# A scan kernel's GpSimd pacing: the wait names the VectorE instruction two places ahead of a multiply-add, not one, where the nearer one is a clip or a tap

## Chip, cores and metric

One Trainium2 chip, one of its cores. The metric is the device time of one launch in microseconds (us); lower is better.

## What is computed

Input x is 8 batches of 1024 tokens with 512 features, cond_2048 is one row of 1024 styles per batch. Two layers are added to x in turn. The first is a style-modulated attention of 16 heads. The second is a gated scan, and the change lies in it:

```python
xr, gate = jnp.split(x @ W_in.T, 2, axis=-1)
xr = xr + t_emb[:, None, :]
xc = silu(causal depthwise conv of 4 taps (xr) + b_conv)
xn = layernorm(xc) * ln_g + ln_b
Bm, Cm, dt = jnp.split(xn @ W_xproj.T, 3, axis=-1)
dt = jnp.tanh(dt @ W_dt.T + b_dt) * 0.01
Ad = 1.0 + dt * A
Bd = Bm * jnp.minimum(norm(xn), 1.0)
def step(h, inputs):
    ad, bd, xt, ct = inputs
    h = jnp.clip(h * ad[:, :, None] + bd[:, :, None] * xt[:, None, :], -10.0, 10.0)
    yt = jnp.einsum('bd,bdh->bh', ct, h)
    return (h, yt)
y = ys + D * xn
return y * silu(gate) @ W_out.T
```

The scan has 1024 steps, one after another; a step updates 16 states x 8 batches x 1024 channels.

## The kernel before

The attention layer comes first and the scan after it. The 8 x 16 pairs of batch and state lie on the 128 partitions, the 1024 channels along a row. The kernel stores h divided by the running product of its decays, so a step needs two VectorE instructions: the **multiply-add** (piece `q`, L2093, g <- xps * bd + g) and the **clip** (piece `g`, L2099, a TENSOR_SCALAR with a minimum and a maximum, in place on g). TensorE spreads the step's input row over the partitions ahead of it (`x`, L1807, into the PSUM tile xps, double buffered), and every fourth step multiplies four clipped states by the expanded C (`out`, L1822).

The 1024 tokens are cut in 8 chunks of 128. While the steps of chunk i run, the engines also prepare chunk i + 1 and finish chunk i - 1. On VectorE that side work is chiefly the **taps** (`tap`, L2106, three of the four of the convolution, each reading xr and cv from SBUF), small statistics (`mu`, `rs`, `rr`, `pjo` at L2161 and L2164, `nmin`, `nmul`) and the last add (`oo`, L2215). All of GpSimd's work in this stage is side work, in pieces of one TENSOR_TENSOR each: `a1`, `a2`, `a3`, `lo` (L2240, L2247, L2255, L2264; the affine part of the layer norm, D * xn, and the low part of a split), `ex` (L2233, the expansion of C, half as wide), `fy` and `fs` (L2272, L2284; the sum with D * xn and the gate). Each of these but `ex` comes as two halves of 512 columns.

The order of the instructions on every engine is laid down before the kernel is built, by the class Order. It keeps a clock of its own for each engine and, while the scan steps are placed, lets a GpSimd piece that is not overdue start only where it would begin within 0.2 of its own units after the start of a multiply-add. `self.open` holds the start of the latest multiply-add and, with it, the VectorE piece that is to be waited for; `place` writes the latter to `plan.pace`. The flag `port` marks the taps, the clips and all GpSimd pieces. When the instructions are emitted, `pace` adds the wait as the last of the piece's own waits:

```python
if p in self.plan.pace:
    for name in self.dve_signals(self.plan.pace[p]):
        w.wait_ge(self.sem[name], self.plan.after(name, self.plan.pace[p]))
```

The semaphores are dve_q for a multiply-add, dve_g for a clip, dve_tap for a tap. Of the 896 GpSimd pieces of the scan 691 are paced. The others follow on the piece before them with their data waits alone.

Of the kernel before, what the change touches and what calls it, by code (L numbers as in the profile page):

```python
# [48 lines left out]
class Plan:  # L49
# [3 lines left out]
    def __init__(self, nc, ctx, name):  # L53
        self.nc, self.ctx, self.name = nc, ctx, name
        self.pieces, self.place, self.counts, self.sems = [], {}, {}, {}
# [50 lines left out]
class Order:  # L106
# [5 lines left out]
    def __init__(self, plan, banks, lag):  # L112
        self.plan, self.lag = plan, lag
        self.now = dict.fromkeys(self.ENGINES, 0.0)
        self.free = dict.fromkeys(range(banks), 0.0)
        self.done, self.lanes, self.step = {}, [], -1

        self.port, self.open, self.before, self.late = {"DVE": 0.0, "POOL": 0.0}, None, None, None

    def lane(self, items, first=None, last=None):

        queues = {e: deque() for e in self.ENGINES}
        whole = sum(item["took"] for item in items) or 1.0
        sofar = 0.0
        for item in items:
            if first is not None:
                item["due"], item["side"] = first + (last - first) * sofar / whole, True
            sofar += item["took"]
            queues[item["engine"]].append(item)  # L130
        self.lanes.append(queues)
# [49 lines left out]
    def place(self, item, engine, start):  # L181
        plan, piece, group = self.plan, item["piece"], item["group"]
        if item["take"] is not None:
            m = min((m for m in item["take"] if self.free[m] is not None), key=lambda m: self.free[m])
            plan.bank[group], self.free[m] = m, None
        m = plan.bank.get(group)
        plan.put(piece, [(name.format(m=m), by) for name, by in item["signals"]])
        end = start + item["took"]
        if engine == "POOL" and self.late is not None and self.open is not None:
            plan.pace[piece], self.open = self.open[1], None  # L190
        if item["port"]:
            self.port[engine] = end
        if item["step"] is not None and engine == "DVE":
            self.open = (start, self.before)
        if engine == "DVE":
            self.before = piece
        self.now[engine] = end
        self.done[piece] = (engine if not item["lands"] else "DMA", end + item["lands"])
        if item["give"]:
            self.free[m] = end + self.lag[item["side"]]  # L200
        if item["step"] is not None:
            self.step = max(self.step, item["step"])
# [2174 lines left out]
```

## Time and profile before

| what | value |
|---|---|
| median of 3 runs | 6171.38 us (6165.83 to 6179.17) |
| profiled execution | 6177.47 us |
| its span | 6175.7 us |
| granted TensorE clock, mean | 0.968 |
| busy shares of the span: TensorE, VectorE, GpSimd, ScalarE | 93%, 73%, 52%, 39% |
| the 1024 steps | 3330.8 to 6087.0 us |

A busy share is the time in which an engine ran an instruction. A row of the timeline gives an instruction's start and duration, and in brackets how long its engine had idled before it and what ended that. An instruction that waits for the memory port while it is under way shows as a longer duration, not as idle time. Rows of the same kind that follow closely are merged (x2, x3), with the time from the first start to the last end.

### The profile page before, as it was taken

The numbers are of one execution on the slowest core, as the hardware profiler recorded it, in microseconds if no ns is written. First come the engines' busy times: TensorE is split into PE (matmuls) and PEld (weight loads), VectorE is DVE, ScalarE is ACT, GpSimd is POOL, SyncE is SP. The second block draws the span as 40 slices with busy tenths as digits, with TensorE's granted clock in tenths as the row PEclk, the third lists the DMA queues.
The fourth block names the chain that finished last, engine by engine and source line by source line (L and its number), as shares of the span: only waits on it lengthen the run. The fifth ranks groups of instructions, "written<-read, shape, count | busy, mean of one in ns | idle before, by whom it ended". The sixth has DMA issues, their size and how long they took to land.

```text
span 6175.7 us, 73238 instructions
## 1 busy us (share of the span) xinstructions
PE 5759.9 (93%) x24000; PEld 2733.8 (44%) x24000; DVE 4481.3 (73%) x5676; ACT 2408.7 (39%) x4698; POOL 3215.3 (52%) x2625
## 2 busy tenths in 40 slices
PE   7999999999999999999986879899999999999998
PEld 3444444444444444444443424444444444444444
DVE  4656656556566565665536999999989999989984
ACT  2444444445444444444453414333342424334111
POOL 1876767677667776776644333425243443524213
PEclk7999999999999999999988889999999999999999
DMA  2332323332232322323214343544444453444433
GB/s 86 89 92 69 100 74 93 91 88 86 79 96 78 98 81 74 98 76 86 91 48 128 84 116 99 141 101 131 109 119 130 117 137 90 137 101 130 116 96 118
DMA packets 411565, 613.30 MB, mean 99 GB/s; under 512 B 58768, under 2 KB 189968, under 8 KB 410672
## 3 DMA queue, kind: packets, MB, share of 16 engines
q1 hardware_dynamic: 374320, 558.24, 32.5%
q10 hardware_dynamic: 36864, 50.38, 3.2%
q8 instruction: 190, 3.11, 0.2%
q14 instruction: 191, 1.56, 0.1%
HBM read 305.31 MB, written 201.38 MB: 82 GB/s over the span
## 4 chain that ended last, share of the span: by engine, by line
PE 67%; DVE 19%; issue 6%; ACT 2%; ACTq 2%; DMA 2%; POOL 1%; DVEq 1%; SPq 1%; POOLq 0%
DVE g L2093 9%; PE bank L786 8%; PE bank L816 8%; PE bank L774 6%; PE misc L803 5%; PE miscb L1832 5%; DVE g L2099 5%; PE xps L1807 5%; PE miscb L1862 4%; PE yps L1822 4%; PE miscb L1764 3%; PE bank L745 3%; PE bank L727 3%; PE bank L755 3%; PE bank L803 2%
## 5 line engine op out<-in xcount | busy, mean ns | idle before, releaser
L1127 POOL TENSOR_TENSOR acc<-acc,prob 128x512 f32<-128x512 f32 x1536 | 1908.1, 1281 | 841.2 <-PE bank L816 571.2
L1056 DVE TENSOR_REDUCE mx<-bank 128x1 f32<-128x512 f32 x2048 | 1307.5, 684 | 538.7 <-PE bank L786 532.4
L2093 DVE SCALAR_TENSOR_TENSOR g<-xps,bd,g 128x1024 f32<-128x1024 f32 x1024 | 1312.9, 1282 | 111.4 <-PE xps L1807 84.1
L1807 PE MATMUL xps<-sx,spread 128*128 128x512 f32 x2048 | 890.3, 520 | 193.9 <-DVE g L2093 180.5
L949 ACT ACTIVATE prob<-misc 128x512 f32<-128x512 f32 x1277 | 713.5, 598 | 751.4 <-PE misc L803 667.8
L786 PE MATMUL bank<-khat,qhat 96*128 96x512 f32 x2048 | 939.4, 519 | 13.2 <-DVE xt_s L1033 8.0
L2099 DVE TENSOR_SCALAR g<-g,lim 128x1024 f32<-128x1024 f32 x1024 | 899.2, 878 | 34.9
L1807 PEld LDWEIGHTS xps<-sx,spread 128*128 128x128 f32 x2048 | 357.7, 194 | 679.3 <-issue 358.4
L803 PE MATMUL misc<-qhat,khat 98*128 98x512 f32 x1443 | 604.1, 461 | 16.9 <-ACT prob L949 10.7
L786 PEld LDWEIGHTS bank<-khat,qhat 96*128 96x128 f32 x2048 | 373.1, 191 | 540.8 <-issue 382.3
L1822 PE MATMUL yps<-g,cexp 128*32 128x512 f32 x4096 | 517.4, 625 | 0.0
L774 PE MATMUL bank<-xhT,wqk 128*128 128x512 f32 x1024 | 490.7, 606 | 2.6 <-ACT rsum L955 1.7
L816 PE MATMUL bank<-prob,V 128*32 128x512 f32 x3584 | 488.4, 615 | 0.2 <-ACT prob L949 0.2
L1764 PE MATMUL miscb<-x2T_sb,w_in 128*128 128x512 f32 x952 | 472.1, 606 | 12.0 <-DMA x2T_sb<-scratch_x2T 12.0
L1862 PE MATMUL miscb<-w_out,ygT 128*128 128x512 f32 x944 | 467.4, 604 | 0.3 <-ACT ygT L2033 0.3
L2233 POOL TENSOR_TENSOR cexp<-cd,mask 128x256 f32<-128x256 f32 x128 | 79.0, 617 | 713.7 <-DVE g L2099 448.5
L1832 PE MATMUL miscb<-w_in,x2T_t 128*128 128x512 f32 x896 | 439.6, 614 | 3.4 <-ACT xr L1912 1.8
L803 PEld LDWEIGHTS misc<-qhat,khat 98*128 98x128 f32 x1443 | 271.0, 190 | 254.0 <-issue 116.2
L2272 POOL TENSOR_TENSOR early<-early 128x512 f32<-128x512 f32 x118 | 150.4, 1275 | 444.1 <-DVE g L2099 244.5
L1047 DVE SCALAR_TENSOR_TENSOR halves<-bank,qk_dc,halves 128x512 fp32r<-128x512 f32 x128 | 95.3, 744 | 368.5 <-ACT halves L913 368.5
L1075 DVE RECIPROCAL rsum<-rsum 128x512 f32<-128x512 f32 x64 | 214.3, 3349 | 190.7 <-ACT rsum L955 190.7
L1912 ACT ACTIVATE xr<-miscb,temb 128x128 f32<-128x128 f32 x476 | 136.0, 369 | 533.5 <-PE miscb L1764 533.5
(221 smaller groups left out, 7212.6 us busy)
## 6 DMA issues: line engine op xcount, KB each, us to landing
sx<-scratch_xhl SPq DMA_DIRECT2D x512, 128.0 KB, 4.9
scratch_dx<-dx SPq DMA_DIRECT2D x64, 512.0 KB, 3.5
scratch_xhl<-xhi SPq DMA_DIRECT2D x64, 512.0 KB, 5.3
scratch_xhl<-xn SPq DMA_DIRECT2D x64, 512.0 KB, 5.6
scratch_y<-ysb SPq DMA_DIRECT2D x512, 64.0 KB
early<-scratch_dx SPq DMA_DIRECT2D x59, 512.0 KB, 6.2
early<-scratch_y SPq DMA_DIRECT2D x59, 512.0 KB, 4.3
xt_n<-in_x SPq DMA_DIRECT2D x112, 256.0 KB, 3.0
```

Of the source, the lines that this page charges most:

```text
L774: mm = pe.matmul(bank[m][:, 0:QC], self.wqk[:, n, it, :], self.xhT[:, it, c * QC:(c + 1) * QC], start=it == 0, stop=it == HT - 1)
L786: pe.matmul(bank[m][:, 0:QC], self.qhat[0:96, s, h, qt * P:(qt + 1) * P], self.khat[0:96, s, h, c * QC:(c + 1) * QC], start=True, stop=Tru ...
L803: pe.matmul(bank[m][:, 0:QC], self.khat[0:98, s, h, kt * P:(kt + 1) * P], self.qhat[0:98, s, h, c * QC:(c + 1) * QC], start=True, stop=Tru ...
L816: mm = pe.matmul(bank[6 + a][h * DH:(h + 1) * DH, 0:QC], self.value(b, kt, g)[:, h * DH:(h + 1) * DH], of, start=kt == 0, stop=kt == TT - 1)
L1056: dve.tensor_reduce(self.mx2[:, h * TT + qt, c:c + 1], bank[m][:, 0:QC], AX.X, ALU.max).then_inc(sem[f"dve_m{m}"], 1)
L1127: pool.tensor_tensor(self.acc[:, a, h, :], self.acc[:, a, h, :], self.prob[:, (n % 2) * GH + h, :], ALU.add).then_inc(sem["pool_acc"], 1)
L1807: mm = pe.matmul(self.xps[t % 2][:, half * BANK:(half + 1) * BANK], self.spread[:, 2 * part + half, :], self.sx[:, n % 2, wd, :], start=Tr ...
L1822: mm = pe.matmul(bank[2 + m][32 * j:32 * (j + 1), :], self.cexp[:, h, tc, :], self.g[:, (t + tp) % STATES, half * BANK:(half + 1) * BANK], ...
L1832: mm = pe.matmul(bank[m][:, :], self.room[rm]["x2T"][:, it, :], self.w_in[:, it, c:c + BANK], start=it == 0, stop=it == HT - 1)
L1862: mm = pe.matmul(bank[m][:, :], self.room[rm]["ygT"][:, ct, :], self.w_out[:, ct, :], start=ct == 0, stop=ct == CT - 1)
L2093: dve.scalar_tensor_tensor(self.g[:, t % STATES, :], self.xps[t % 2][:, :], self.bd[:, i % 2, tl:tl + 1], self.g[:, (t - 1) % STATES, :], ...
L2099: dve.tensor_scalar(self.g[:, t % STATES, :], self.g[:, t % STATES, :], self.lim[:, i % 2, 0, tl:tl + 1], self.lim[:, i % 2, 1, tl:tl + 1] ...
```

## The change

The planner now remembers, beside the last VectorE piece (`before`), the one ahead of it (`held`) where the last one is a clip or a tap. A multiply-add's entry names `held` if there is one.

```diff
@@ Order.__init__
         self.port, self.open, self.before, self.late = {"DVE": 0.0, "POOL": 0.0}, None, None, None
+        self.held = None
@@ Order.place
         if item["step"] is not None and engine == "DVE":
-            self.open = (start, self.before)
+            self.open = (start, self.held or self.before)
         if engine == "DVE":
+            self.held = self.before if item["port"] else None
             self.before = piece
```

Nothing in the choice of the next piece reads the name, so the order of instructions is the same on all five engines; only GpSimd's waits differ. Of the 691 paced pieces 520 named a clip. Of those 479 now name the multiply-add ahead of that clip, the one that the clip itself waits for; 19 name a projection (`pjo`), 18 a tap, 3 an output add, 1 a variance. Of the 65 that named a tap, 40 now name the tap ahead of it, 18 a clip and 7 a minimum.

GpSimd's rows, first a place within chunk 3 (in the trace it begins at 4499.38 us). Before:

```order
L2284 TENSOR_TENSOR early<-early,sg 128x512 [waits s_dve_g,s_pool_y0,s_act_m1]
L2240 TENSOR_TENSOR xn<-xn,affine 128x512 [waits s_act_nm]
L2240 TENSOR_TENSOR xn<-xn,affine 128x512 [waits s_dve_g]
L2247 TENSOR_TENSOR xn<-xn,affine 128x512 [waits s_dve_tap,s_pool_x] x2
L2255 TENSOR_TENSOR dx<-xn,affine 128x512 [waits s_dve_g,s_st_dx,s_pool_x]
L2255 TENSOR_TENSOR dx<-xn,affine 128x512 [waits s_dve_g,s_pool_x]
L2233 TENSOR_TENSOR cexp<-cd,mask 128x256 [waits s_dve_g,s_pe_y]
L2264 TENSOR_TENSOR xn<-xn,xhi 128x512 [waits s_pool_x,s_dve_tap,s_act_sq,s_act_hi]
L2264 TENSOR_TENSOR xn<-xn,xhi 128x512 [waits s_pool_x]
L2240 TENSOR_TENSOR xn<-xn,affine 128x512 [waits s_dve_g,s_act_nm]
L2240 TENSOR_TENSOR xn<-xn,affine 128x512 [waits s_dve_g]
```

After (the changed file's lines stand two further down):

```order
L2286 TENSOR_TENSOR early<-early,sg 128x512 [waits s_dve_q,s_pool_y0,s_act_m1]
L2242 TENSOR_TENSOR xn<-xn,affine 128x512 [waits s_act_nm]
L2242 TENSOR_TENSOR xn<-xn,affine 128x512 [waits s_dve_tap]
L2249 TENSOR_TENSOR xn<-xn,affine 128x512 [waits s_dve_g,s_pool_x]
L2249 TENSOR_TENSOR xn<-xn,affine 128x512 [waits s_dve_tap,s_pool_x]
L2257 TENSOR_TENSOR dx<-xn,affine 128x512 [waits s_dve_q,s_st_dx,s_pool_x]
L2257 TENSOR_TENSOR dx<-xn,affine 128x512 [waits s_dve_q,s_pool_x]
L2235 TENSOR_TENSOR cexp<-cd,mask 128x256 [waits s_dve_q,s_pe_y]
L2266 TENSOR_TENSOR xn<-xn,xhi 128x512 [waits s_pool_x,s_dve_tap,s_act_sq,s_act_hi]
L2266 TENSOR_TENSOR xn<-xn,xhi 128x512 [waits s_pool_x]
L2242 TENSOR_TENSOR xn<-xn,affine 128x512 [waits s_dve_q,s_act_nm]
L2242 TENSOR_TENSOR xn<-xn,affine 128x512 [waits s_dve_q]
```

No row has moved. Where dve_g stood there is dve_q in seven rows and dve_tap in one, and the number of waits of each of these rows is what it was: three for the first halves of `a3` and `fs`, two for `ex` and the second half of `a3`, one for the second half of `a1`.

VectorE's rows of a step, the same before and after:

```order
L2099 TENSOR_SCALAR g<-g,lim 128x1024 [waits s_dve_q]
L2093 SCALAR_TENSOR_TENSOR g<-xps,bd,g 128x1024 [waits s_pe_xps,s_dve_g]
L2099 TENSOR_SCALAR g<-g,lim 128x1024 [waits s_dve_q]
```

The clip's only wait is for dve_q, the semaphore that 479 GpSimd pieces now wait for too.

Among these 479 pieces 80 have that one wait alone (41 `a1`, 26 `fy`, 13 `ex`), 217 have two waits (39 `a1`, 64 `a2`, 36 `a3`, 14 `lo`, 64 `ex`), and 182 have three or four (41 `a3`, 73 `fs`, 44 `fy`, 24 `lo`).

## Rows read from the trace of the kernel before

**Rows 1.** The page: span, then busy us, share and instructions of engines.
```profile
span 6175.7 us, 73238 instructions
PE 5759.9 (93%) x24000; PEld 2733.8 (44%) x24000; DVE 4481.3 (73%) x5676; ACT 2408.7 (39%) x4698; POOL 3215.3 (52%) x2625
```

**Rows 2.** Windows: the steps; PE, PEld, DVE, ACT, POOL busy us, PEclk, DMA, GB/s.
```profile
3330.80:6087.00 2756.20, 2542.69 (x10754) 1208.58 (x10754) 2532.09 (x2747) 921.52 (x1926) 950.60 (x798) 0.97 0.43 113
```

**Rows 3.** Groups of VectorE and TensorE in the window of the steps.
```profile
L2093 DVE SCALAR_TENSOR_TENSOR g<-xps,bd,g 128x1024 f32<-128x1024 f32 x1024 | 1312.9, 1282 | 111.4 <-PE xps L1807 84.1 <-DVE g L2099 0.2
L2099 DVE TENSOR_SCALAR g<-g,lim 128x1024 f32<-128x1024 f32 x1024 | 899.2, 878 | 34.9
L1807 PE MATMUL xps<-sx,spread 128*128 128x512 f32 x2046 | 889.3, 520 | 180.8 <-DVE g L2093 180.5
```

**Rows 4.** VectorE's waits in that window: us in total, times, longest.
```profile
DVE g L2093 <- PE xps L1807: 84.1, 66, 9.4
DVE proj L2161 <- PE miscb L1783: 56.3, 24, 2.9
DVE x_t L2215 <- PE miscb L1862: 17.4, 13, 1.9
```

**Rows 5.** Timeline 4511 to 4518 us, VectorE and GpSimd.
```profile
4512.79 1.28 DVE L2093 SCALAR_TENSOR_TENSOR g<-xps,bd,g 128x1024 f32<-128x1024 f32 x1
4512.93 1.28 POOL L2255 TENSOR_TENSOR dx<-xn,affine 128x512 f32<-128x512 f32 x1 [0.80 <-DVE g L2099]
...
4514.11 0.81 DVE L2099 TENSOR_SCALAR g<-g,lim 128x1024 f32<-128x1024 f32 x1
...
4514.96 1.28 DVE L2093 SCALAR_TENSOR_TENSOR g<-xps,bd,g 128x1024 f32<-128x1024 f32 x1
4515.07 1.28 POOL L2255 TENSOR_TENSOR dx<-xn,affine 128x512 f32<-128x512 f32 x1 [0.86 <-DVE g L2099]
```

**Rows 6.** Timeline at 4526 us, a piece whose lone wait is the clip.
```profile
4526.49 1.28 DVE L2093 SCALAR_TENSOR_TENSOR g<-xps,bd,g 128x1024 f32<-128x1024 f32 x1
4526.53 1.28 POOL L2240 TENSOR_TENSOR xn<-xn,affine 128x512 f32<-128x512 f32 x1 [0.63 <-DVE g L2099]
```

**Rows 7.** Who waited for the clip, first and last of seven: us, times.
```profile
  POOL cexp L2233: 448.5, 71
...
  POOL dx L2255: 64.4, 70
```

**Rows 8.** Timelines at two places where clip and GpSimd start together.
```profile
3927.80 1.84 DVE L2099 TENSOR_SCALAR g<-g,lim 128x1024 f32<-128x1024 f32 x1
...
3927.81 1.27 POOL L2272 TENSOR_TENSOR early<-early 128x512 f32<-128x512 f32 x1
...
4849.58 1.93 DVE L2099 TENSOR_SCALAR g<-g,lim 128x1024 f32<-128x1024 f32 x1
4849.68 1.28 POOL L2284 TENSOR_TENSOR early<-early,sg 128x512 f32<-128x512 f32 x1
```

**Rows 9.** Timeline where GpSimd starts later than in rows 8.
```profile
3442.55 0.81 DVE L2099 TENSOR_SCALAR g<-g,lim 128x1024 f32<-128x1024 f32 x1
3442.69 3.04 POOL L2255 TENSOR_TENSOR dx<-xn,affine 128x512 f32<-128x512 f32 x2
```

**Rows 10.** Timelines of a clip behind an earlier full piece, and behind `ex`.
```profile
4524.63 1.27 POOL L2240 TENSOR_TENSOR xn<-xn,affine 128x512 f32<-128x512 f32 x1
...
4524.89 1.56 DVE L2099 TENSOR_SCALAR g<-g,lim 128x1024 f32<-128x1024 f32 x1
...
4642.69 0.61 POOL L2233 TENSOR_TENSOR cexp<-cd,mask 128x256 f32<-128x256 f32 x1
4642.95 0.90 DVE L2099 TENSOR_SCALAR g<-g,lim 128x1024 f32<-128x1024 f32 x1
```

## The prediction

> **What bounds the kernel now.** I read the page first: TensorE is busy for 93% of the span and VectorE for 73%, GpSimd for 52% [rows 1]. The change touches only the stage of the 1024 steps, so that stage has to be read by itself. Its window is 2756.2 us long; VectorE is busy for 2532.1 of it and TensorE for 2542.7, GpSimd for 950.6 [rows 2]. Two engines are thus full to 92%, and GpSimd has two thirds of its time free. What GpSimd does can cost time only by being late or by standing in another engine's way.
>
> Which of the two full engines waits for the other decides what a lost microsecond on VectorE costs. TensorE stood idle 180.5 us for the multiply-adds [rows 3]. VectorE waited 84.1 us in 66 waits for the rows that TensorE spreads, 56.3 us in 24 for the projections and 17.4 us in 13 for the output products [rows 4]; that is 158 us in 103 waits over 1024 steps. So in most steps VectorE waits for nobody: an undisturbed step is a multiply-add of 1.28 us, 0.03 to 0.04 us, a clip of 0.81 us and again 0.04 us, 2.17 us in all [rows 5], and a delay there moves every later step.
>
> The timeline shows how GpSimd is paced. The clip that starts at 4514.11 ends at 4514.92. The multiply-add follows at 4514.96, GpSimd's piece at 4515.07, and the two run side by side in 1.28 us each, neither one stretched [rows 5]. The piece ends at 4516.35, about 0.07 us into the next clip, which still takes its 0.81 us.
>
> How far GpSimd starts behind the multiply-add depends on how many waits its piece has, though the same clip releases both. With the clip as its lone wait it is 0.04 us [rows 6], with two waits 0.11 us, with three 0.14 us (4512.79 and 4512.93) [rows 5].
>
> **What the change does at a step.** It adds and removes no instruction of work and moves none. 479 pieces are released by the end of a multiply-add in place of the clip behind it. That same end releases the clip, and the clip's gap is the multiply-add's: 34.9 us over 1024 clips, 0.034 us [rows 3]. So I carry the three offsets over: the piece will start 0.04, 0.11 or 0.14 us behind a *clip*, with one, two, or three and more waits. Then it matters who gets the memory port.
>
> The rows show it. Where a piece starts 0.01 us or 0.10 us behind a clip, the clip takes 1.84 and 1.93 us in place of 0.81 and the piece its usual 1.27 or 1.28 [rows 8]: although the clip started first, GpSimd went first. In the steps 38 clips have a piece that starts up to 0.10 us behind them; all 38 were held, and the two places in rows 8 are the first and the last of them by offset. Where the piece starts 0.14 us behind, the clip keeps its 0.81 us and it is the piece that stretches (two pieces take 3.04 us) [rows 9]; that and 7 more clips with an offset up to 0.18 us were not held. The border lies between 0.10 and 0.14 us.
>
> The Trainium skill ("SBUF — State Buffer", section "SBUF: two separate sides") calls the shared pair of ports an exclusive lock: the instruction that starts first has it for its whole length and the other fully blocks. Of the blocking the trace agrees (1.93 in place of 0.81 us). Of who wins, the recorded starts disagree with it in all 38 cases.
>
> **The price of one held clip.** From rows 8, 1.84 - 0.81 = 1.03 us at 0.01 us and 1.12 at 0.10: 1.02 plus the offset. For the half-wide `ex` I compare at one offset: 0.26 us ahead of a clip, a full piece makes it 1.56 us and `ex` 0.90 [rows 10], so `ex` costs 0.66 us less.
>
> - One wait, offset 0.04: 67 full pieces at 1.06 and 13 `ex` at 0.40: 76 us. This offset lies well inside the held ones.
> - Two waits, offset 0.11: 153 at 1.13 and 64 at 0.47: 203 us. This lies 0.01 above the last held row and 0.03 below the first free one; I take it as held.
> - Three and more, offset 0.14: 182 at 1.16: 211 us. This lies at the first free row; I take it as not held.
>
> Not every piece is released by its pacing wait. The profile names the clip as what ended the wait of 467 pieces (seven rows, first and last in [rows 7]) of 520 that name one, 0.90. So 0.90 x (76 + 203) = 251 us.
>
> **What comes off.** The present conflicts cost (0.878 - 0.81) x 1024 = 70 us [rows 3]. Half of them are those 38 clips, hit by a piece that follows at once on a paced one. If the first of such a pair has three or four waits it now starts under the clip, blocked, and runs from the clip's end, about 0.3 us earlier than now. Its follower starts as much earlier and meets the next clip from 0.26 us ahead, which makes it 1.56 us in place of about 1.87 [rows 8, 10]: 38 x 0.3, some 10 us saved at the most. That leaves 241 us.
>
> **What is absorbed.** VectorE's 158 us of waits [rows 4] can swallow delays that came up before them, if TensorE goes on meanwhile; it cannot where it waits for the multiply-add itself. Nothing swallowed (241 us) and all 158 swallowed (83 us) are the bounds. The waits are few and the conflicts spread over all chunks, so I take a quarter: 181 us.
>
> Edits costed at nothing: the 19 clips after a projection, 18 after a tap and 3 after an output add do not wait for the piece named, and are under way when GpSimd comes; if they were held too, 40 x 1.1 = 44 us. The 18 that go from a tap to a clip come behind a tap that is under way likewise. The 40 with a tap behind a tap have offsets of 0.11 or 0.14 again, but no row shows who wins there; from nothing to 33 x 1.13 + 7 x 0.47 = 41 us. I take nothing and keep it for the top. GpSimd itself has two thirds of its time free, and nobody waits longer for its pieces than it now gains.
>
> **Sum.** The profiled execution took 6177.47 us; with 181 it is 6358, and the median is 6 us below that execution: 6352. I say 6350 us.
>
> **The rivals.**
>
> - *Only the lone waits collide* (the border is below 0.11 us). 0.90 x 76 - 10 = 58 us, less a quarter: 44 us, 6215 us. For it: no held row lies above 0.10 us.
> - *All collide* (the border is above 0.14 us). 0.90 x 490 = 441 us. The second pieces of pairs then find their clip over, which takes 38 x 1.06 = 40 off; three quarters of 401 is 301: 6472 us, and 6610 if nothing is swallowed. Against it: the clip was free at 0.14 us [rows 9].
> - *The clip always wins, the kernel is faster.* A clip and a piece released by one semaphore might be served in the order of their starts. Then no clip is lengthened, GpSimd starts at the clip's very end, 0.1 to 0.2 us earlier than now, and ends before the next clip begins. The gain is a part of the 70 us of conflicts; a third of it gives 6148 us, all of it 6101. This decides if no clip is held at 0.04 us. The skill's sentence above (first start has the port) is this rival, for 0.03 is less than 0.04. Against it stand all 38 rows.
> - *Nothing to be seen*: the pieces come after other waits so often, or the delays are swallowed so fully, that it stays at 6171 us. Against it are the 467 releases [rows 7] and the 103 waits only [rows 4].
>
> **How the numbers follow.** Two waits held and three not, my forecast: 0.5. Only lone waits: 0.2, all: 0.2, since the first has a fifth of the gap between 0.10 and 0.14 us below its offset and the last sits at the border. The clip wins: 0.06. Nothing: 0.04. The forecast's own range is 6270 (most swallowed, 83 us) to 6435 (nothing swallowed). The range reaches down to the lone-wait case, a little below 6215, and up through the middle of the all-held case: 6200 to 6510 us. It leaves out the two last rivals and the top of the second, some 2 in 10. A difference of under 0.2%, 12 us, can't be told from none here. Slower by more: 0.90; within: 0.05; faster by more: 0.05.
>
> **What the changed profile would show.** The clip's mean up from 878 ns: with 241 us more, to about 1110; to 935 if only lone waits collide, 1270 if all do, and below 878 if the clip wins. The second half of `a1` and of `fy` 0.04 us behind a clip of 1.87 us. Pieces with three waits stretched to about 1.8 us, with a clip of 0.81 us beside them. VectorE's 158 us of waits down by some 60, TensorE's 180.5 us of waiting for multiply-adds up. ScalarE and the 3330.8 us ahead of the steps as before. I am wrong at the root if clips keep 0.81 us beside a piece that starts 0.04 us behind them; wrong in size if the border is elsewhere or TensorE proves to be the real bound, so that more than half is swallowed.

## The result and the profile after

The changed kernel takes 6224.32 us (6213.63 to 6230.46), the kernel before 6172.0 us in the same comparison: a ratio of 1.0083, 95% interval 1.0065 to 1.01, 52 us slower. Slower was forecast, at 6350 us: the time lies in the range of 6200 to 6510, but the loss is less than a third of the 178 us that I gave. It lies 9 us above the first rival's 6215 us, and the range holds it only because it was stretched down to that rival: the forecast's own range began at 6270.

The page of the changed kernel, then its window of the steps (TensorE, weight loads, VectorE, ScalarE, GpSimd, granted clock, DMA, GB/s):

```profile
span 6228.6 us, 73238 instructions
...
PE 5796.9 (93%) x24000; PEld 2741.4 (44%) x24000; DVE 4527.1 (73%) x5676; ACT 2407.2 (39%) x4698; POOL 3436.1 (55%) x2625
```
```profile
3335.40:6140.60 2805.20, 2566.58 (x10756) 1212.76 (x10754) 2586.92 (x2746) 920.46 (x1926) 1172.97 (x798) 0.96 0.42 111
```

The window is 2805.2 us long; before it was 2756.2 [rows 2]: of the 52.9 us by which the span grew, 49 lie in it and 4.6 ahead of it. The start of the steps lies anywhere between 3321.5 and 3335.5 us in the eleven profiles, whatever the names. VectorE is busy for 54.8 us more there, GpSimd for 222 us more, and both engines ran the same instructions over the kernel.

The groups of the changed kernel in that window, with the same columns as [rows 3]:

```profile
L2095 DVE SCALAR_TENSOR_TENSOR g<-xps,bd,g 128x1024 f32<-128x1024 f32 x1024 | 1312.9, 1282 | 117.1 <-PE xps L1809 89.6
L2101 DVE TENSOR_SCALAR g<-g,lim 128x1024 f32<-128x1024 f32 x1024 | 954.4, 932 | 34.9
...
L1809 PE MATMUL xps<-sx,spread 128*128 128x512 f32 x2047 | 890.3, 521 | 208.3 <-DVE g L2095 207.3
```

The multiply-adds take what they took, and the gap ahead of the clips is the same 34.9 us. The clips alone grew, by 55.2 us, from 878 to 932 ns in the mean. TensorE waited 207.3 us for the multiply-adds, 27 us more than before. VectorE's waits for TensorE, to be held against [rows 4], add up to 153 us, 5 less than before:

```profile
DVE g L2095 <- PE xps L1809: 89.6, 68, 9.2
DVE proj L2163 <- PE miscb L1785: 50.0, 24, 2.9
DVE x_t L2217 <- PE miscb L1864: 13.0, 8, 2.1
```

Which clips grew is in the timeline. Three places of the changed kernel, VectorE and GpSimd:

```profile
4176.62 0.81 DVE L2101 TENSOR_SCALAR g<-g,lim 128x1024 f32<-128x1024 f32 x1
4176.75 1.82 POOL L2257 TENSOR_TENSOR dx<-xn,affine 128x512 f32<-128x512 f32 x1 [0.23 <-DVE g L2095]
...
4178.78 0.81 DVE L2101 TENSOR_SCALAR g<-g,lim 128x1024 f32<-128x1024 f32 x1
4178.89 1.85 POOL L2257 TENSOR_TENSOR dx<-xn,affine 128x512 f32<-128x512 f32 x1 [0.32 <-DVE g L2095]
...
4190.45 1.88 DVE L2101 TENSOR_SCALAR g<-g,lim 128x1024 f32<-128x1024 f32 x1
4190.49 1.29 POOL L2242 TENSOR_TENSOR xn<-xn,affine 128x512 f32<-128x512 f32 x1 [0.27 <-DVE g L2095]
```

All three pieces were released by the end of a multiply-add. With three waits (the first half of an `a3`) the piece starts 0.13 us behind the clip (4176.75), with two (the second half) 0.11 us (4178.89): the clip keeps its 0.81 us, and the piece is the one that stretches, from 1.28 to 1.82 or 1.85 us. With one wait (the second half of an `a1`) it starts 0.04 us behind the clip (4190.49): the clip takes 1.88 us. Over the whole kernel 69 clips have a piece 0.04 us behind them and are held, and of the 283 with an offset of 0.105 to 0.135 us not one is. The last held offset of the two kernels is 0.098 us, the smallest free one 0.105.

The balance of the clips, each against 0.81 us: the 69 cost 65.6 us. The clips held by a follower 0.01 to 0.10 us behind them fell from 38 to 6, those held by a piece that had started ahead of them or otherwise rose from 44 to 69; together these two give 10.4 us back. 65.6 - 10.4 = 55.2 us.

### The profile page after: what moved, and what is told of

Read it like the earlier page. It is cut to its first block, busy times and chain, and to the rows that moved or that the text cites. A ratio compares the mean times of both kernels' runs of the same rounds, so it can differ in the third digit from the quotient of the medians.

```text
span 6228.6 us, 73238 instructions
## 1 busy us (share of the span) xinstructions
PE 5796.9 (93%) x24000; PEld 2741.4 (44%) x24000; DVE 4527.1 (73%) x5676; ACT 2407.2 (39%) x4698; POOL 3436.1 (55%) x2625
## 4 chain that ended last, share of the span: by engine, by line
PE 62%; DVE 23%; issue 6%; ACT 2%; ACTq 2%; DMA 2%; POOL 1%; DVEq 1%; SPq 1%; POOLq 0%
DVE g L2095 11%; PE bank L788 8%; PE bank L818 8%; DVE g L2101 6%; PE bank L776 6%; PE misc L805 5%; PE miscb L1834 4%; PE xps L1809 4%; PE yps L1824 3%; PE bank L747 3%; PE miscb L1864 3%; PE bank L729 3%; PE bank L757 3%; DVE cv L2108 2%; PE miscb L1766 2%
## 5 line engine op out<-in xcount | busy, mean ns | idle before, releaser
L1809 PE MATMUL xps<-sx,spread 128*128 128x512 f32 x2048 | 890.8, 521 | 221.2 <-DVE g L2095 207.3
L2101 DVE TENSOR_SCALAR g<-g,lim 128x1024 f32<-128x1024 f32 x1024 | 954.4, 932 | 34.9
L2235 POOL TENSOR_TENSOR cexp<-cd,mask 128x256 f32<-128x256 f32 x128 | 116.7, 912 | 674.4 <-DVE g L2095 415.3
L2274 POOL TENSOR_TENSOR early<-early 128x512 f32<-128x512 f32 x118 | 170.6, 1448 | 425.2 <-DMA early<-scratch_y 244.4
```

What stands on the lines that cost most here:

```text
L1809: mm = pe.matmul(self.xps[t % 2][:, half * BANK:(half + 1) * BANK], self.spread[:, 2 * part + half, :], self.sx[:, n % 2, wd, :], start=Tr ...
L2101: dve.tensor_scalar(self.g[:, t % STATES, :], self.g[:, t % STATES, :], self.lim[:, i % 2, 0, tl:tl + 1], self.lim[:, i % 2, 1, tl:tl + 1] ...
```

## The experiments

Two facts of the code are needed for them.
**Without the lone waits (e1).** `near` holds the name of before. Here and below only the lines that decide are shown.

```diff
         if p in self.plan.pace:
-            for name in self.dve_signals(self.plan.pace[p]):
-                w.wait_ge(self.sem[name], self.plan.after(name, self.plan.pace[p]))
+            named = self.plan.pace[p] if w.fresh else self.plan.near[p]
+            for name in self.dve_signals(named):
+                w.wait_ge(self.sem[name], self.plan.after(name, named))
```

> The changed kernel, but a piece whose pacing wait would be its only wait keeps the name of before (the clip); all others are as changed. First theory: the whole loss comes from lone-wait pieces that start 0.04 us behind a clip and take the port from it (69 held clips, some 55 us of clip time). Then no clip is held at 0.04 us, the clip's mean is back at 870 to 885 ns and the time at 6160 to 6180 us. Rival: the loss comes from the 300 pieces with two and more waits, which now start under a clip and run on from its end, so that their followers meet the next clip from ahead; then the time stays within 15 us of 6224.

6152.38 us, ratio to before 0.9979 (0.997 to 0.9988). The clip's mean was 869 ns. The first theory holds and its rival falls: the other pieces that now name the multiply-add, 217 with two waits and 182 with more, cost nothing. They even gain 17 us, so that the time lies 8 us below the range expected.

**The offset alone (e2, e9).** All names as changed; only the lone pieces get one more wait, on a load that landed long ago.

```diff
         if p in self.plan.pace:
+            if not w.fresh:
+                w.engine.wait_ge(self.sem["ld_const"], 48)
             for name in self.dve_signals(self.plan.pace[p]):
```

> The changed kernel with one more wait, long satisfied (on the constants' load), called ahead of the pacing wait where that was the only one. First theory: the offset decides. The pacing wait then stands in an instruction of its own and the piece starts 0.11 us behind the clip in place of 0.04; it loses the port, no clip is held there, 6155 to 6180 us, clip mean 865 to 885 ns. Rival: naming the multiply-add costs by itself, whatever the offset: 6224 us.

6151.16 us, ratio 0.9972 (0.996 to 0.9983), against 6224 without the extra wait. The second half of an `a1` in this kernel, a piece of the kind that starts at 4190.49 above:

```profile
4162.01 0.81 DVE L2104 TENSOR_SCALAR g<-g,lim 128x1024 f32<-128x1024 f32 x1
4162.12 1.84 POOL L2246 TENSOR_TENSOR xn<-xn,affine 128x512 f32<-128x512 f32 x1 [0.33 <-DVE g L2098]
```

0.11 us in place of 0.04, and the clip keeps its 0.81 us. An added wait that is already met thus makes the kernel some 72 us faster (6222.99 us for e3, run beside it): the offset decides, not the name. One thing stays open. In e2, e3 and e5 the offset changes together with the instruction that holds the pacing wait, so for pieces that wait the two are not told apart. For the offset itself speak the followers, which wait for nothing when they start: they are held from 0.01 to 0.10 us and free from 0.14 us on.

**The same wait at the other place (e3).** It is called behind the pacing wait.

```diff
             for name in self.dve_signals(self.plan.pace[p]):
                 w.wait_ge(self.sem[name], self.plan.after(name, self.plan.pace[p]))
+            if w.fresh == 1:
+                w.engine.wait_ge(self.sem["ld_const"], 48)
```

> As the run with the satisfied wait ahead, but it is called behind the pacing wait, so the pacing wait stays the one that the work instruction itself holds. If what counts is which wait the instruction holds, these pieces still start 0.04 us behind the clip, the 69 clips stay held and the time is 6215 to 6235 us. If the number of waits counts, the offset is 0.11 us and the time 6155 to 6180 us.

6222.99 us, ratio 1.0091 (1.0076 to 1.0106), the changed kernel's time. In this kernel:

```profile
4184.09 1.88 DVE L2104 TENSOR_SCALAR g<-g,lim 128x1024 f32<-128x1024 f32 x1
4184.14 1.29 POOL L2246 TENSOR_TENSOR xn<-xn,affine 128x512 f32<-128x512 f32 x1 [0.26 <-DVE g L2098]
```

As many waits as in e2, yet the offset is 0.04 us (0.042 to 0.044 before rounding). What counts is not how many waits a piece has but where the pacing wait stands among them.

**The lone pieces alone (e4).** The names of e1 the other way round.

```diff
+            named = self.plan.near[p] if w.fresh else self.plan.pace[p]
```

> The opposite part alone: only pieces whose pacing wait is their only wait name the instruction two places ahead, all others the clip or tap as before. First theory: about 69 clips held at 0.04 us, 57 full ones at 1.06 us and 12 half-wide ones at 0.40, 65 us of clip time less what else shifts: 6220 to 6240 us. Rival (the others cost): 6172 us.

6234.63 us, ratio 1.0111 (1.0096 to 1.0126), as expected. 88 clips were held by a piece 0.04 to 0.06 us behind them, against 26 in the kernel before, and the clips took 957.2 us against 899.2. Here the others name the clip again and do not give their small gain, which is why I take this kernel to be slower than the changed one, by 12 us against e3. The loss of the lone pieces is some 65 to 73 us, seen from either side.

**All pieces at 0.04 us (e5).** `pace` is called ahead of every other wait of the piece.

```diff
         for p in plan.pieces:
             kind, *at = p
+            self.pace(w, p)
...
-                self.pace(w, p)
```

> The changed kernel with the pacing wait called first for every GpSimd piece, so that the work instruction itself holds it, however many waits the piece has. If that wait is what makes the piece start 0.04 us behind the clip, nearly all 430 to 479 clips are now held: against the changed kernel 0.9 x (335 x 1.06 + 64 x 0.40) = 340 us more of clip time, mean near 1250 ns, and with a tenth of it swallowed about 6530 us (6450 to 6570). It also measures how much of a large delay TensorE's slack swallows: a quarter would give 6480, nothing 6565. Rival (the number of waits sets the offset): 6224 us, clip mean 932 ns.

6532.67 us, ratio 1.0589 (1.0573 to 1.0605). This is what it costs when all collide: it lies between the 6472 us of that rival and its 6610. It is also what was expected of the run. The piece is at 0.04 us although it has two or three waits, and both prices of the prediction can be read off. A half-wide `ex`, then a full `fs`:

```profile
4151.54 1.21 DVE L2101 TENSOR_SCALAR g<-g,lim 128x1024 f32<-128x1024 f32 x1
4151.58 0.62 POOL L2235 TENSOR_TENSOR cexp<-cd,mask 128x256 f32<-128x256 f32 x1 [12.48 <-DVE g L2095]
...
4174.30 1.87 DVE L2101 TENSOR_SCALAR g<-g,lim 128x1024 f32<-128x1024 f32 x1
4174.34 1.28 POOL L2280 TENSOR_TENSOR early<-early,sg 128x512 f32<-128x512 f32 x1 [1.95 <-DVE g L2095]
```

1.87 - 0.81 = 1.06 us and 1.21 - 0.81 = 0.40 us, as priced. 363 clips were held at 0.04 us. The groups and waits of this kernel in the steps (waits: us in total, times, longest):

```profile
L2101 DVE TENSOR_SCALAR g<-g,lim 128x1024 f32<-128x1024 f32 x1024 | 1247.5, 1218 | 34.9
L2108 DVE SCALAR_TENSOR_TENSOR cv<-xr,wconv,cv 128x512 f32<-128x512 f32 x336 | 296.9, 884 | 7.5 <-ACT cv L1924 0.9
```
```profile
DVE g L2095 <- PE xps L1809: 70.6, 49, 9.1
DVE proj L2163 <- PE miscb L1785: 52.8, 24, 3.0
DVE x_t L2217 <- PE miscb L1864: 10.9, 6, 1.9
```

Clips took 348 us more than before [rows 3] and taps 40 us more (296.9 against 257.0 in the kernel before). VectorE's waits for TensorE fell from 158 us [rows 4] to 134: of 388 us 24 were swallowed, 6%. The time agrees, 365 us more.

**Naming the unpaced pieces too (e6).** As e2, and a piece that follows at once on another names the latest multiply-add placed (`self.last`).

```diff
-        if engine == "POOL" and self.late is not None and self.open is not None:
-            plan.pace[piece], self.open = self.open[1], None
+        if engine == "POOL" and self.late is not None:
+            if self.open is not None:
+                plan.pace[piece], self.open = self.open[1], None
+            elif self.last is not None:
+                plan.pace[piece] = self.last
```

> The changed kernel with the satisfied wait ahead of lone pacing waits, and with a pacing wait for the pieces that have none now (they follow at once on the piece before): they name the latest multiply-add placed. No clip should then find a piece that started 0.26 us ahead of it or 0.04 behind it. The 73 other held clips of the changed kernel cost some 60 us of clip time; if most of them go, the clip's mean falls to 815 to 840 ns and the time to 6110 to 6140 us, below both kernels. Rival: pieces that wait become late, and TensorE and the output products wait for them; then 6170 us or more, with VectorE's or TensorE's waits up.

6147.71 us, ratio 0.9965 (0.9952 to 0.9978). The fastest of the first six by its median, but within the spread of e1 and e2, and not the 6110 to 6140 expected. The clip's mean fell to 849 ns only: 54 clips still meet a piece that started about 0.26 us ahead of them. Such a place, shown in e2, where it occurs likewise:

```profile
4179.59 0.81 DVE L2104 TENSOR_SCALAR g<-g,lim 128x1024 f32<-128x1024 f32 x1
4179.73 1.81 POOL L2290 TENSOR_TENSOR early<-early,sg 128x512 f32<-128x512 f32 x1
...
4181.50 1.28 POOL L2261 TENSOR_TENSOR dx<-xn,affine 128x512 f32<-128x512 f32 x1
4181.76 1.57 DVE L2104 TENSOR_SCALAR g<-g,lim 128x1024 f32<-128x1024 f32 x1
```

The first piece is stretched by a clip and ends at 4181.54; the next, whose release is past, is recorded from 4181.50, just as that one ends. This is 0.26 us ahead of the next clip, and that takes 1.57 us.

**One multiply-add for each piece (e7).** In the same place; `self.prior` is the name of the piece before.

```diff
+            named, self.open = (self.open[1], None) if self.open is not None else (self.last, None)
+            if named is not None:
+                if self.prior is not None and plan.place[named] <= plan.place[self.prior]:
+                    named = self.last
+                plan.pace[piece] = self.prior = named
```

> The kernel in which all pieces are named, with one rule more: a piece whose name lies no later in the plan than the name of the piece before it names the latest multiply-add placed. In the version without the rule 54 clips are still hit by a piece that started about 0.26 us ahead of them. Theory: these are pieces behind a backlog; their name was long past, so they started on the heels of the piece before. With the rule they wait for a multiply-add of their own: held clips 10 to 30, clip mean 820 to 835 ns, VectorE 15 to 30 us shorter, 6115 to 6135 us. Rival: GpSimd's pieces then come later and the waits of TensorE and VectorE for the chunk's side work grow by as much: 6140 to 6155 us with a clip mean just as low.

6177.5 us, ratio 1.0012 (1.0003 to 1.0021): slower than e6 by some 30 us, and not as expected. The clip's mean did fall, to 835 ns, but the taps gave it back, and VectorE waited more. First e6, then e7, in the steps:

```profile
L2108 DVE TENSOR_SCALAR g<-g,lim 128x1024 f32<-128x1024 f32 x1024 | 869.1, 849 | 34.9
L2115 DVE SCALAR_TENSOR_TENSOR cv<-xr,wconv,cv 128x512 f32<-128x512 f32 x336 | 263.4, 784 | 6.3
```
```profile
L2109 DVE TENSOR_SCALAR g<-g,lim 128x1024 f32<-128x1024 f32 x1024 | 855.0, 835 | 34.9
L2116 DVE SCALAR_TENSOR_TENSOR cv<-xr,wconv,cv 128x512 f32<-128x512 f32 x336 | 282.9, 842 | 6.9 <-ACT cv L1932 0.6
```

Clips 14 us less, taps 19.5 us more: 33 taps were held in the steps, against 13. VectorE's waits for the rows of TensorE rose from 89.3 to 99.4 us, and 7.8 us of waits for ScalarE's sum of squares are new. That is 5.4 us of clips and taps and 18 us of waits; some 6 of the 30 us stay unexplained. Neither theory had the time. The rival named the waits, which are the larger part, and nobody the taps. Which of the later pieces met which tap I did not follow up.

**Is it the names that gain? (e8, e9).** e8 is the kernel of before with e2's three lines; e9 is e2 again, on the same chip.

> The kernel of before, all names as they were, with the satisfied wait ahead of lone pacing waits. Theory: the 18 us that the changed names gain once the lone pieces no longer take the port come from the names, so here nothing moves: 6160 to 6176 us, clip mean 870 to 885 ns. Rival: they come from the 0.07 us later start of the lone pieces; then this kernel too is at 6145 to 6155 us.

> The changed names with the satisfied wait ahead once more, beside the kernel of before with that wait, to have both on one chip: 6145 to 6160 us, and 10 to 25 us below the other.

e8: 6164.32 us, ratio 0.9993 (0.9984 to 1.0002), no difference. e9: 6146.67 us, ratio 0.9969 (0.996 to 0.9979), 18 us below e8. So the changed names gain about 0.3% once no lone piece takes the port from a clip, and the extra wait gains nothing by itself.

## Why the prediction was right in its mechanism and wrong in its size

- **"The piece will start 0.04, 0.11 or 0.14 us behind a clip"**: right. After, they start 0.04, 0.11 and 0.13 us behind it. The offsets carry over from the multiply-add to the clip.
- **The lone waits, 80 pieces, 76 us**: right. 69 clips were held, at 1.06 us a full piece and 0.40 an `ex` (e5), 65.6 us in all. With the cut of 0.90 the term was 68 us; e1, e2 and e4 put it at 65 to 73 us of time.
- **"Two waits, offset 0.11: ... I take it as held"**: this step failed. The term of 203 us was nothing: the pieces with two waits came 0.11 us behind the clip, and all those clips kept their 0.81 us. The offset stood 0.01 us above the last held row and 0.03 below the first free one, and I went by the nearer row. No row of before lay in that gap; the border is between 0.098 and 0.105 us. The nearer row was also of another kind, a piece that followed on its predecessor without idling, while the pieces of this term are released by a wait. Without this term the sum is the first rival's, 44 us against the 52 measured. The forecast's 0.5 against 0.2 for the right case came from treating the border as equally likely anywhere in it.
- **Three and more waits, not held**: right. They were free at 0.13 us, and e5 shows that the same pieces are held when they come at 0.04.
- **What comes off, 10 us**: right, 10.4 us in the changed kernel. In e2, where only this is left, the clips' mean falls from 878 to 861 ns, 17 us, while the taps take 6.5 us more. The followers now meet a clip from 0.26 us ahead (1.57 us) and not from 0.01 to 0.10 behind (1.84 to 1.93). That kernel gains 19 us (e2) and 23 us (e9) against before; the 11 us of clips and taps explain half, and what makes up the rest stays open. Within the steps VectorE idled 2 us less in the profile of e2 and 12 us less in that of e9.
- **"I take a quarter"** as swallowed: too much. From before to after the clips grew by 55 us and the steps by 49, and VectorE's waits fell by 5 us, not by the 60 foretold; in e5 VectorE gave up 24 us of waits for 388 us of delays, where a quarter would be 97.
- **Two sums are off.** The bounds of 83 and 241 us on the median of 6171 give 6254 and 6412, not 6270 and 6435. And the 6610 of the second rival leaves out the 40 us that its 6472 takes off; with them it is 6572. Neither moves the forecast.
- **The taps behind a tap, taken at nothing**: right for the changed kernel; those with an offset of 0.11 and 0.13 us kept their 0.75 us, one `ex` at 0.045 us held its tap to 1.21 us, and the taps' total in the steps is 257.6 us against 257.0. In e5, where the same offset is 0.04, they took 40 us more.
- **The rival in which the clip always wins, and the sentence of the Trainium skill** ("SBUF — State Buffer", section "SBUF: two separate sides") that who starts first has the port: 0.04 us behind, GpSimd still went first, 69 times here and 363 times in e5. That one of the two waits for the other holds, though not to the full recorded length: the clip from 4190.45 ends 0.55 us after the piece, less than its own 0.81, and the piece from 4178.89 ends 1.15 us after its clip, less than its own 1.28. The order of the recorded starts is not the order in which the two were served; that turns over at about 0.1 us.

## What to carry to other kernels

When two engines are released by one event and contend for one port, ask not only who starts first but by how much: here a few hundredths of a microsecond decided about 1 us a clip. The place of a wait among an instruction's waits sets that offset, so a long satisfied wait ahead of the pacing wait can buy it: here it turns 52 us lost into some 20 us won. Where a forecast hangs on a border that the trace brackets only loosely, its two sides are two forecasts, and the nearest row counts only if it is of the same kind.

## What the runs showed of the hardware that I had not expected

- A GpSimd piece starts 0.079 us after the end of the VectorE instruction that releases it if its own instruction holds that wait. If the wait stands in a sequencer instruction ahead, it is 0.145 us where it stands there alone (e2) and mostly 0.17 us where another stands with it. The order in which the waits are called decides which one the instruction holds, not their number (e3, e5).
- The border between clip and piece lies between 0.100 and 0.105 us of recorded start over the traces of all eleven profiled runs, without an exception: 0.100 costs the clip 1.11 us, 0.105 nothing. But every held row above 0.045 us is a piece that followed on its predecessor (GpSimd had idled 0.04 us at most). For a piece that had waited longer the last held offset is 0.045 us and the first free one 0.105, so where its own border lies between them is not shown.
- For a tap one place does not fit this border: in e8 a piece starts 0.077 us behind a tap that keeps its 0.75 us, and the piece takes 1.81 us. It is the only such place, so where the border of a tap lies is not shown.
- A blocked GpSimd piece loses little. Stretched to 1.85 us from 4178.89, it ends at 4180.74, 1.15 us after its clip, while a piece released by that clip would start 0.14 us after it and run 1.28: 0.27 us later.
